# The second expert mixture of a small vision tower: rows sent through DRAM by number, or moved on the chip by 0/1 matrix products

## The chip, the cores and the metric

The kernel runs on one core of a Trainium2 chip. The metric is the time of one execution on the device in microseconds (us), as a median of several runs. Matrix products run on TensorE (PE in the profile, its weight loads as PEld), the rest on VectorE (DVE), ScalarE (ACT) and GpSimd (POOL); SyncE (SP) issues DMAs only. Each engine works off its own list of instructions in order, and semaphores tie the lists together.

## The reference

32 images of 64x64 become 17 tokens of 128 numbers each, so 544 tokens (T). Two layers follow, each of attention and a mixture of experts. The change lies in the last part, the second mixture: 32 experts, the best two for each token, and at most CAP = 43 tokens for one expert (slots are given in token order).

```python
C = int(np.ceil(CAPACITY_FACTOR * BTK / N))          # 1.25 * 1088 / 32 -> 43
probs = jax.nn.softmax(x_flat @ Wg, axis=-1)
vals, idx = jax.lax.top_k(probs, K)                  # K = 2
vals = vals / jnp.clip(vals.sum(-1, keepdims=True), 1e-09)
rank = jnp.cumsum(oh, axis=0) - oh                   # place within the expert
keep = pos < C
dest = jnp.where(keep, a * C + pos, N * C)
buf = jnp.zeros((N * C, D), x.dtype).at[dest].set(x_flat[token], mode='drop')
h = jax.nn.relu(jnp.einsum('ncd,ndh->nch', buf, W1) + b1[:, None, :])
o = (jnp.einsum('nch,nhd->ncd', h, W2) + b2[:, None, :]).reshape(N * C, D)
y_flat = jax.ops.segment_sum(gathered * w[:, None], token, num_segments=BT)
y_flat = jnp.where(contrib[:, None] <= 1e-12, x_flat, y_flat)
```

The layer's output is the residual `h` plus `y_flat`.

## The kernel before

All tokens lie on the chip in G = 5 groups g of 119 (the last of 68), tokens on the partitions: `h` is the residual, `xm[:, g, 0]` the normalised rows (`xm[:, g, 1]` a copy). The order of the work is written out by hand, per engine, in `sp`, `pool`, `act`, `dve` and `pe` blocks.

**Router stage** (about 146 to 167 us of the profile). For each group PE makes the attention's output product (`project`, 16 instructions of the profile), DVE adds it to `h` and takes the statistics (`attended`, `stats`), POOL (groups 0 and 1, by a power) or ACT (groups 2 to 4, by a root) gives the inverse deviation, DVE writes `xm` (`normalised3`), PE turns it (`router_turn`), ACT copies it out, PE makes the 32 logits (`router_logits`), DVE finds the two best and marks them (`pick2`, `mark2`), PE counts ranks (`slot_ranks`) and DVE reads the slot number off (`place2`). Between these PE runs products of a constant tile, `fill(...)`, that compute nothing that is used.

**Way out.** `scatter2` on POOL (L587) sends each row of `xm` twice, by an indirect DMA, to the DRAM buffer `rooms2` at its slot; a row carries its pair's number with it. SP waits for all ten scatters and reads `rooms2` back into `xb2` in three pieces (L480). While these are under way PE runs 32 fillers.

**Pair stage** (175 to 202 us). PAIRS = 16 pairs of experts; for each pair j PE turns the slots (`pair_turned`, L1788), DVE copies (`slots_in`, L1296), PE multiplies by the two first matrices (`pair_up`), ACT adds the bias and takes the positive part in two instructions (`rectified`, L824), PE multiplies by the two second matrices (`pair_down`), DVE adds the bias (`pair_biased`, L1301) and POOL scatters the 112 result rows to `o_rows` in DRAM (`spread_rows2`, L595).

**Way back** (203 to 214 us). SP and ACT read `o_rows` in token order (L380 to L387), DVE weights and adds the two rows of a token (L1314, L1323), five stores leave from SP and ACT (L489, L835 and others).

Every product in float32 shows as two MATMUL instructions in the trace, so a `pair_up` or `pair_down`, which is two products, shows as x4. All products made with the helper `mm` have line L1330.

## Time and profile before

| | |
|---|---|
| time, median of 3 runs | 210.02 us (209.72 to 211.75) |
| span of the profiled execution | 214.1 us, 3836 instructions |
| busy | PE 84%, PEld 63%, DVE 47%, POOL 37%, ACT 34% |
| from the first router pick to the first `pair_up` | 150.80 to 175.35 us |
| pair stage, first `pair_up` to last bias | 175.35 to 201.99 us |
| way back and stores | 202 to 214.1 us |

A time of its own is not given for the profiled execution beside its span; the span is the time from its first to its last instruction and is 4.1 us above the median of the runs. A sum of changes is therefore made on the span and then taken off or added to the median. Rows of the trace name line, engine, operation, tiles, shapes and count; the first two numbers are start and duration in us, and square brackets hold the idle time ahead on that engine and what ended it.

### The profile page before, as it was taken

The page shows a single profiled execution, that of the slowest core. Times are in us where ns is not written, and L with a number is a line of the kernel's source. Part 1 is how long each engine was busy: PE and PEld are TensorE (multiplying, and loading weights), DVE is VectorE, ACT ScalarE, POOL GpSimd, SP SyncE. Part 2 cuts the span into 40 slices and gives each one's busy share as a digit, 9 for nine tenths or more (in the row PEclk, how much of TensorE's full clock was granted, in tenths as well). Part 3 has the DMA queues.
Part 4 walks back from the last instruction along what each step waited for, and adds up shares of the span by engine and source line. Part 5 has one row for each costly group of instructions (what it writes and reads, how often), then busy time and mean ns, then how long its engine had stood idle before and what let it go on. Part 6 is the DMA issues. An engine that isn't in the chain of part 4 may idle for free.

```text
span 214.1 us, 3836 instructions
## 1 busy us (share of the span) xinstructions
PE 179.6 (84%) x1347; PEld 135.6 (63%) x1351; DVE 101.6 (47%) x373; ACT 73.2 (34%) x219; POOL 79.4 (37%) x104
## 2 busy tenths in 40 slices
PE   6979799989899899999999889968787969986400
PEld 2946467777687699999687565457664436655200
DVE  0037676978453127882217618363446713333104
ACT  2002253543425445665510554083214002332100
POOL 8008341500875037886502300001156602565510
PEclk9995999996558999999999999979999985998855
DMA  6959999980121429981140179940011153111142
GB/s 183 291 156 307 367 294 346 368 350 5 36 52 26 101 57 318 301 327 40 37 119 4 48 225 428 318 112 0 3 33 37 38 118 48 42 34 35 32 124 53
DMA packets 18956, 31.12 MB, mean 145 GB/s; under 512 B 4838, under 2 KB 12517, under 8 KB 18554
## 3 DMA queue, kind: packets, MB, share of 16 engines
q1 hardware_dynamic: 15552, 27.15, 39.5%
q0 software_dynamic: 2784, 3.31, 6.0%
q10 hardware_dynamic: 602, 0.42, 0.7%
q8 instruction: 11, 0.18, 0.3%
q14 instruction: 7, 0.06, 0.1%
HBM read 23.52 MB, written 7.40 MB: 144 GB/s over the span
## 4 chain that ended last, share of the span: by engine, by line
PE 53%; POOL 12%; DMA 12%; issue 11%; DVE 5%; ACT 2%; SPq 2%; POOLq 1%; ACTq 0%; DVEq 0%
PE ps L1330 50%; POOL rooms L587 5%; DMA patchesT<-in_patchesT 4%; POOL rooms L549 4%; DMA xb<-rooms 2%; POOL o_rows L595 2%; DVE xn L866 2%; POOL ln_rstd L525 2%; PE ps L1788 1%; DMA o_tok<-o_rows 1%; DMA rooms<-xm,slot 1%; DMA rooms<-xm,room 1%; DMA o_rows<-o_sb,result_row 1%; SPq L411 1%; PE ps L1575 1%
## 5 line engine op out<-in xcount | busy, mean ns | idle before, releaser
L556 POOL DMA_INDIRECT o_rows<-o_sb,result_row x16 | 21.0, 1312 | 18.1 <-DVE o_sb L1073 15.7
L525 POOL TENSOR_TENSOR ln_rstd<-ln_var,minus_half 119x1 f32<-119x1 f32 x12 | 6.7, 566 | 51.3 <-DVE ln_var L860 51.3
L728 ACT ACTIVATE hid_b<-ps,w_ring 128x128 f32<-128x128 f32 x64 | 18.3, 369 | 14.2 <-PE ps L1330 13.4
L595 POOL DMA_INDIRECT o_rows<-o_sb,result_row x16 | 15.1, 943 | 18.7 <-DVE o_sb L1301 15.6
L549 POOL DMA_INDIRECT rooms<-xm,room x10 | 11.4, 1144 | 15.8 <-issue 15.8
L1330 PE MATMUL ps<-w_ring,hid_b 128*128 128x128 f32 x128 | 17.0, 276 | 0.3 <-ACT hid_b L728 0.3
L1330 PE MATMUL ps<-xbT,w_ring 128*128 128x128 f32 x128 | 17.0, 275 | 0.0
L1330 PE MATMUL ps<-filler 128*128 128x512 bf16 x51 | 15.4, 433 | 1.7 <-DVE filler L878 1.5
L824 ACT ACTIVATE hid<-ps,moe_b 128x64 f32<-128x64 f32 x32 | 8.3, 311 | 24.0 <-PE ps L1330 18.6
L1330 PEld LDWEIGHTS ps<-w_ring,hid_b 128*128 128x128 f32 x128 | 15.6, 192 | 0.5 <-ACT hid_b L728 0.5
L1330 PEld LDWEIGHTS ps<-xbT,w_ring 128*128 128x128 f32 x128 | 15.6, 192 | 0.0
L1330 PE MATMUL ps<-x2T,m 128*128 128x128 f32 x64 | 12.7, 334 | 2.9 <-DVE x2T L1296 2.9
L587 POOL DMA_INDIRECT rooms<-xm,slot x10 | 11.0, 1095 | 9.5 <-DVE slot L1222 7.4
L1330 PEld LDWEIGHTS ps<-x2T,m 128*128 128x128 f32 x64 | 11.5, 251 | 3.8 <-DVE x2T L1296 3.5
L905 DVE TENSOR_TENSOR sd<-ps,decay 119x476 f32<-119x476 f32 (+1 forms) x20 | 10.8, 602 | 3.1 <-PE ps L1330 2.9
L1301 DVE TENSOR_TENSOR o_sb<-ps,moe_b 128x128 f32<-128x128 f32 x16 | 4.5, 290 | 16.3 <-PE ps L1330 14.4
L1073 DVE TENSOR_TENSOR o_sb<-ps,b_all 128x128 f32<-128x128 f32 x16 | 4.7, 291 | 15.1 <-PE ps L1330 12.4
L1330 PE MATMUL ps<-xT,w_s 128*128 128x272 f32 x32 | 11.8, 538 | 0.0
L1330 PE MATMUL ps<-w_f,heldT 128*119 128x128 f32 (+1 forms) x80 | 11.1, 297 | 0.0
L1330 PEld LDWEIGHTS ps<-filler 128*128 128x128 bf16 x55 | 6.1, 116 | 6.9 <-issue 1.7
L1330 PEld LDWEIGHTS ps<-w_f,heldT 128*119 128x119 f32 (+1 forms) x80 | 10.1, 194 | 0.4 <-issue 0.3
L613 ACT COPY xT<-ps 128x119 f32<-128x119 f32 (+1 forms) x15 | 3.6, 253 | 19.7 <-PE ps L1340 13.3
(209 smaller groups left out, 361.8 us busy)
## 6 DMA issues: line engine op xcount, KB each, us to landing
w_ring<-in_w_routed SPq DMA_DIRECT2D x16, 514.0 KB
m<-in_m SPq DMA_DIRECT2D x2, 2048.0 KB, 13.0
rooms<-zeros SPq DMA_DIRECT2D x8, 330.0 KB, 5.4
patchesT<-in_patchesT SPq DMA_DIRECT2D x6, 272.0 KB, 5.3
xb<-rooms SPq DMA_DIRECT2D x16, 66.0 KB
w_s<-in_w_s SPq DMA_DIRECT2D x2, 512.0 KB, 5.9
moe_b<-in_moe_b SPq DMA_DIRECT2D x2, 512.0 KB, 16.9
rooms<-zeros SPq DMA_DIRECT2D x1, 792.0 KB, 6.7
```

Of the source, the lines that this page charges most:

```text
L525: nc.gpsimd.tensor_tensor(ln_rstd[:, g:g + 1], ln_var[:, g:g + 1], minus_half[:], ALU.pow).then_inc(rstd_ready, 1)
L549: nc.gpsimd.indirect_dma_start(rooms[:], bass.IndirectOffsetOnAxis(ap=room[0:n, g, k:k + 1], axis=0), xm[0:n, g, k, :], None).then_inc(sca ...
L556: nc.gpsimd.indirect_dma_start(o_rows[:], bass.IndirectOffsetOnAxis(ap=result_row[:, b:b + 1], axis=0), o_sb[:, b, :], None).then_inc(o_sc ...
L587: nc.gpsimd.indirect_dma_start(rooms2[:], bass.IndirectOffsetOnAxis(ap=slot[0:n, g, k:k + 1], axis=0), xm[0:n, g, k, :], None).then_inc(sc ...
L595: nc.gpsimd.indirect_dma_start(o_rows[:], bass.IndirectOffsetOnAxis(ap=result_row2[0:past_, j:j + 1], axis=0), o2_sb[0:past_, j, :], None) ...
L728: nc.scalar.activation(hid_b[:, b % RING, c, :], ps[:, b % 2, c * BS:(c + 1) * BS], ACT.Gelu, bias=w_ring[:, b % WRING, FF + c:FF + c + 1] ...
L824: nc.scalar.activation(hid2[:, e, :], ps[:, 2 + j % 2, at:at + ROOM], ACT.Relu, bias=moe_b1[:, e:e + 1]).then_inc(hid2_ready, 1)
L866: nc.vector.tensor_scalar(xn[:, g, 0:width], h[:, g, 0:width], mv[:, g, 0:1], ln_rstd[:, g:g + 1], ALU.subtract, ALU.mult).then_inc(xn_rea ...
L905: nc.vector.tensor_tensor(sd[0:n, g % 2, r, :, :, 0:n], src, decay[0:n, r, :, 0:n].unsqueeze(2).to_broadcast([n, 2, 2, n]), ALU.mult).then ...
L1073: nc.vector.tensor_tensor(o_sb[:, b, :], ps[:, 4 + b % 2, 0:D], bias, ALU.add).then_inc(block_out, 1)
L1301: nc.vector.tensor_tensor(o2_sb[:, j, :], ps[:, 4 + j % 2, 0:D], moe_b2[:, j, :], ALU.add).then_inc(o2_ready, 1)
L1330: return nc.tensor.matmul(out_, lhsT, rhs, start=first, stop=last)
```

## The change

Rows of tokens no longer go through DRAM. What changes, part by part:

- **Slots by product.** `slots_marked` (DVE) compares, for each group, a table of slot numbers (32 experts x RS = 44 places) with each token's slot: one 119x1408 array of 0 and 1 (`in_slot`). `gather` (PE) multiplies the tokens with it, into three PSUM banks (484, 484 and 440 columns) over all groups. So that a product with 0/1 is exact, the tokens are split in two parts of type float32r, `x_hi` (ACT) and `x_lo` (POOL): 6 products a group. DVE and ACT copy the three banks to `x2T`.
- **Weights early.** The weights of a token's two experts are made group by group (`top_gap`, `gap_exponent`, `top_weights`), and `scatter2` now sends a record of 16 numbers (token number and weight) instead of a row; two loads bring the records back as `rec_in`, a row for each slot.
- **Back by product.** For pair j, ACT scales the result and rounds it (`result_high`), DVE makes the rest (`result_low`) and a 128x544 array of 0/1 from the token numbers (`tokens_marked`); PE adds both parts times that array (`pair_summed`: 238, 238, 306, 306 columns) into two PSUM banks, over all pairs, and the residual too (`residual`). One copy on DVE and one on ACT, one store each. The output is now laid out as 128x544.
- **Order of the pair stage.** Six `pair_up` and four `pair_down` come ahead; then for each j: `pair_down(j + 4)`, `pair_up(j + 6)`, `pair_summed(j)`. On ACT: `rectified(j + 6)`, `result_high(j)`. On DVE: `pair_biased(j + 4)`, `tokens_marked(j)`, `result_low(j)`.
- **Gone:** `rooms2` and its zeroing, the reload `xb2`, all turns of pairs, the 16 scatters to `o_rows` and the read back, all fillers of the stage, ACT's roots (POOL makes all five powers). **Moved or new elsewhere:** one more load on POOL's queue (`slot_base`, 4th of a row of loads near 20 us), two zeroings, two small and two broadcast loads on SP, two PSUM banks for `project`.

```diff
 (pool)
             load("room_base", room_base[:], dram["room_base"])
+            load("slot_base", slot_base[:], dram["slot_base"])
...
-            nc.gpsimd.memset(xb2[:], 0.0).then_inc(xb2_zero, 1)
+            nc.gpsimd.tensor_scalar(before16[:], before[:], 16.0, None, ALU.mult).then_inc(pool_set, 1)
+            nc.gpsimd.tensor_scalar(ones16[:], ones[:], 16.0, None, ALU.mult).then_inc(pool_set, 1)
...
+            rstd(3, (0, 1))
+            low_part(0)
+            rstd(3, (2,))
+            scatter2(0)
...
+            scatter2(3)
+            scatter2(4)
-            for j in range(PAIRS):
-                spread_rows2(j)
 (act)
-            for j in range(PAIRS):
-                rectified(j)
+            def result_high(j):
+                act.wait_ge(o2_ready, j + 1)
+                act.wait_ge(slot_w_ready, 1)
+                nc.scalar.activation(o2_hi[:, j, :], o2_sb[:, j, :], ACT.Copy,
+                                     scale=slot_w[:, j:j + 1]).then_inc(o2_hi_ready, 1)
+            for j in range(AHEAD):
+                rectified(j)
+            for j in range(PAIRS):
+                if j + AHEAD < PAIRS:
+                    rectified(j + AHEAD)
+                result_high(j)
 (dve)
+            def slots_marked(g):
+                if g >= 2:
+                    dve.wait_ge(gathered, g - 1)
+                dve.wait_ge(at_ready, g + 1)
+                nc.vector.tensor_tensor(in_slot[0:n, g % 2], slot_pos[0:n],
+                                        picked_at[0:n, g, :].unsqueeze(2).to_broadcast([n, EM, RS]),
+                                        ALU.is_equal).then_inc(in_slot_ready, 1)
+            def result_low(j):
+                dve.wait_ge(o2_hi_ready, j + 1)
+                nc.vector.scalar_tensor_tensor(o2_lo[:, j, :], o2_sb[:, j, :], slot_w[:, j:j + 1],
+                                               o2_hi[:, j, :].bitcast(F32), ALU.mult, ALU.subtract).then_inc(o2_lo_ready, 1)
+            for j in range(LATE):
+                pair_biased(j)
+            dve.wait_ge(rec_loaded, 32)
+            nc.vector.tensor_scalar(slot_w[:], rec_in[:, :, 1], row_kept[:, 0:1], None, ALU.mult).then_inc(slot_w_ready, 1)
+            for j in range(PAIRS):
+                if j + LATE < PAIRS:
+                    pair_biased(j + LATE)
+                tokens_marked(j)
+                result_low(j)
 (pe)
-            fill(FILLS, 6)
+            def pair_summed(j):
+                pe.wait_ge(of_token_ready, j + 1)
+                pe.wait_ge(o2_hi_ready, j + 1)
+                for i, own in enumerate((slice(0, SPLIT), slice(SPLIT, T))):
+                    for part in (o2_hi, o2_lo):
+                        if part is o2_lo and i == 0:
+                            pe.wait_ge(o2_lo_ready, j + 1)
+                        last = nc.tensor.matmul(ps[:, SUM_BANK[i], 0:own.stop - own.start], part[:, j, :],
+                                                of_token[:, j % CRING, own], start=j == 0 and part is o2_hi,
+                                                stop=j == PAIRS - 1 and part is o2_lo)
+            for j in range(PAIRS):
+                if j + AHEAD - 2 < PAIRS:
+                    pair_down(j + AHEAD - 2)
+                if j + AHEAD < PAIRS:
+                    pair_up(j + AHEAD)
+                pair_summed(j)
+                if 1 <= j <= G:
+                    residual(j - 1)
```

Three places of the order, as the built programs have it. First PE's pair stage. Before, pairs 3 and 4; `ps<-ident,xb` is a turn, `ps<-x2T,m` an up, `ps<-m,hid` a down, and the words in brackets are the semaphores waited for (`hid2_ready` from ACT, `x2T_ready` and `o2_ready` from DVE):

```order
L1788 MATMUL ps<-ident,xb 128x128 [waits x2T_ready]
L1330 MATMUL ps<-x2T,m 128x128 [waits hid2_ready,x2T_ready]
L1330 MATMUL ps<-x2T,m 128x128
L1330 MATMUL ps<-m,hid 64x128 [waits o2_ready,hid2_ready]
L1330 MATMUL ps<-m,hid 64x128
```

Now, the down of pair 4, the up of pair 6, the sum of pair 0, and the down of pair 5 behind it:

```order
L1412 MATMUL ps<-m,hid 64x128 [waits o2_ready,hid2_ready]
L1412 MATMUL ps<-m,hid 64x128
L1412 MATMUL ps<-x2T,m 128x44 [waits hid2_ready]
L1412 MATMUL ps<-x2T,m 128x44
L1914 MATMUL ps<-of_token,o_hi 128x238 [waits o2_hi_ready,of_token_ready]
L1914 MATMUL ps<-of_token,o_lo 128x238 [waits o2_lo_ready]
L1914 MATMUL ps<-of_token,o_hi 128x306
L1914 MATMUL ps<-of_token,o_lo 128x306
L1412 MATMUL ps<-m,hid 64x128 [waits o2_ready,hid2_ready]
```

The turns are gone, and between two ups there now stand products that wait for ACT and DVE; a product of the sum is one instruction here, not two.

Second, ACT in the same stage. Before, all 32 halves of `rectified` in a row:

```order
L824 ACTIVATE hid<-ps,moe_b 128x64 [waits up2_done]
L824 ACTIVATE hid<-ps,moe_b 128x64
L824 ACTIVATE hid<-ps,moe_b 128x64 [waits up2_done]
L824 ACTIVATE hid<-ps,moe_b 128x64
L824 ACTIVATE hid<-ps,moe_b 128x64 [waits up2_done]
```

Now, pairs 6 and 7 with the high parts of pairs 0 and 1:

```order
L866 ACTIVATE hid<-ps,moe_b 128x44 [waits up2_done]
L866 ACTIVATE hid<-ps,moe_b 128x44
L873 ACTIVATE o_hi<-o_sb,slot_w 128x128 [waits slot_w_ready,o2_ready]
L866 ACTIVATE hid<-ps,moe_b 128x44 [waits up2_done]
L866 ACTIVATE hid<-ps,moe_b 128x44
L873 ACTIVATE o_hi<-o_sb,slot_w 128x128 [waits slot_w_ready,o2_ready]
```

Behind each pair's two halves now stands the high part of the pair six places back.

Third, DVE in the router stage, from the ranks of group 1 to the pick of group 2. Now:

```order
L1262 TENSOR_TENSOR place_of<-marks,ps 119x64 [waits rank2_done]
L1265 TENSOR_TENSOR picked_at<-place_of 119x32 [waits dve_step]
L1268 TENSOR_REDUCE slot<-place_of 119x2
L1292 TENSOR_SCALAR gap_sum<-gap 119x1 [waits gap_exp]
L1293 RECIPROCAL rec<-gap_sum 119x1 [waits dve_step]
L1294 TENSOR_TENSOR rec<-gap,rec 119x1 [waits dve_step]
L1278 TENSOR_TENSOR in_slot<-slot_pos,picked_at 119x1408 [waits at_ready]
L1246 MAX top<-ps 119x8 [waits logits_done]
```

Before, `place_of`, `slot` and the next pick stood there; the rows L1265, L1292 to L1294 and L1278 are new between them.

## Rows read from the trace of the kernel before

**Rows 1.** The page: span, and TensorE's granted clock in 40 slices.

```profile
span 214.1 us, 3836 instructions
PEclk9995999996558999999999999979999985998855
```

**Rows 2.** Timeline, 19 to 24 us: DVE beside POOL's loads.

```profile
19.84 3.43 DVE L866 TENSOR_SCALAR xn<-h,mv,ln_rstd 119x128 f32<-119x128 f32 x1 [0.17 <-POOL ln_rstd L525]
20.34 0.53 POOL L498 DMA_DIRECT2D ones<-in_ones  x1
21.36 1.82 POOL L560 MEMSET probs<- 128x2048 f32 x1
```

**Rows 3.** Timeline of the router stage.

```profile
150.80 0.20 DVE L1202 MAX8 top<-ps 119x8 f32<-119x32 f32 x1 [1.42 <-PE ps L1330]
153.56 0.19 DVE L1218 TENSOR_TENSOR place_of<-marks,ps 119x64 f32<-119x64 bf16 x1
162.24 0.30 ACT L668 COPY xm<-xm 119x128 f32<-119x128 f32 x1
```

**Rows 4.** Groups by form, DVE: busy us, mean ns.

```profile
L1091 DVE TENSOR_TENSOR q_mixed<-w_t,th_q 128x1024 f32<-128x1024 f32 x4 | 4.9, 1218 | 0.0
L1076 DVE TENSOR_TENSOR w_t<-w_t 128x1524 f32<-128x1524 f32 x1 | 1.7, 1728 | 0.0
L893 DVE TENSOR_SCALAR kT<-xT,parity 128x544 f32<-128x544 f32 x2 | 0.9, 500 | 0.7 <-ACT xT L613 0.7
L895 DVE COPY qT<-ps 128x544 f32<-128x544 f32 x1 | 0.7, 724 | 1.1 <-PE ps L1330 1.1
L1323 DVE SCALAR_TENSOR_TENSOR ymoe<-o_tok,pair_w,h 119x128 f32<-119x128 f32 x4 | 1.4, 345 | 0.0
```

**Rows 5.** Timeline: 512 columns in bf16 (29 in a row) and in float32.

```profile
166.05 5.96 PEld L1330 LDWEIGHTS ps<-filler 128*128 128x128 bf16 x29
104.83 3.60 PE L1330 MATMUL ps<-q_mixed,w_t 128*128 128x512 f32 x8
```

**Rows 6.** Timeline of the records' model: last scatter, reload, first turn.

```profile
169.39 1.11 POOL L587 DMA_INDIRECT rooms<-xm,slot  x1 [0.30 <-issue]
172.30 2.79 SPq L480 DMA_DIRECT2D xb<-rooms  x6
174.63 0.20 PEld L1788 LDWEIGHTS ps<-ident,xb 128*128 128x128 f32 x2 [1.98 <-DMA xb<-rooms]
```

**Rows 7.** Timeline of the pair stage at half clock.

```profile
180.10 0.70 PE L1330 MATMUL ps<-m,hid 128*64 128x128 f32 x4
180.73 0.48 PE L1788 MATMUL ps<-ident,xb 128*128 128x128 f32 x1
181.00 1.06 PE L1330 MATMUL ps<-x2T,m 128*128 128x128 f32 x4
182.10 0.52 ACT L824 ACTIVATE hid<-ps,moe_b 128x64 f32<-128x64 f32 x2 [1.37 <-PE ps L1330]
```

**Rows 8.** The same at full clock.

```profile
184.31 0.44 PE L1330 MATMUL ps<-m,hid 128*64 128x128 f32 x4
184.68 0.33 PE L1788 MATMUL ps<-ident,xb 128*128 128x128 f32 x1
184.85 0.61 PE L1330 MATMUL ps<-x2T,m 128*128 128x128 f32 x4
185.50 0.52 ACT L824 ACTIVATE hid<-ps,moe_b 128x64 f32<-128x64 f32 x2 [0.56 <-issue]
187.49 0.29 DVE L1301 TENSOR_TENSOR o_sb<-ps,moe_b 128x128 f32<-128x128 f32 x1 [2.15 <-PE ps L1330]
```

**Rows 9.** Engines by stretch: us, PE busy (count), granted clock, DMA share, GB/s.

```profile
190.00:194.00 4.00, 2.67 (x23) 1.00 0.15 43
194.00:198.00 4.00, 3.66 (x24) 0.75 0.12 33
```

**Rows 10.** Timeline: the last store.

```profile
211.83 0.36 ACTq L837 DMA_DIRECT2D out_h<-ymoe  x1
```

More of the change, by code:

```diff
@@ L55 @@
 ROOM = 64
+RS = 44
 TAKEN = 48
@@ L427, in _ @@
                              zeros[:, 0:n * RW]).then_inc(rooms_zero, 16)
+            for half in range(2):
+                at = (1 + half) * HALF_STEP
+                sp.dma_start(rec_rows[at:at + TAKEN * REC, :].rearrange("(p r) c -> p (r c)", p=128),
+                             zeros[:, 0:TAKEN * REC * REC // 128]).then_inc(rooms_zero, 16)
             sp.dma_start(w2_s[:], dram["w2_s"]).then_inc(shared_loaded, 16)
@@ L785, in _, with high_part @@
             folded_out(1)
-            nc.scalar.activation(warm[:], eps_col[0:1, 0:1], ACT.Sqrt)
             for grp in range(2, GRPS):
                 held_to(grp)
-            def deviation3(g):
-                act.wait_ge(aggr_ready, 3 * G + g + 1)
-                nc.scalar.activation(ln_std[:, g:g + 1], mv[:, g, 1:2], ACT.Sqrt, bias=eps_col[:, 0:1]).then_inc(std_ready, 1)
+            def high_part(g):
+                n = rows(g)
+                act.wait_ge(xn_ready, 3 * G + g + 1)
+                nc.scalar.copy(x_hi[0:n, g, :], xm[0:n, g, 0, 0:D]).then_inc(hi_ready, 1)
             def router_out(g):
@@ L1231, in _ @@
             softmaxed(3)
+            here(dve, "row_kept", "rec")
             attended(0)
@@ L1317, in _ @@
[L1317 to L1324 removed]
+                nc.vector.tensor_tensor(o2_sb[:, j, :], ps[:, DOWN_BANK[j % 2], 0:D], moe_b2[:, j, :],
+                                        ALU.add).then_inc(o2_ready, 1)
@@ L1706, in slot_ranks, with gather @@
                 pe.wait_ge(picks_ready, G + g + 1)
-                mm(dst, ones[0:1, 0:n], room_base[:, ER:], True, False)
+                mm(dst, ones[0:2, 0:n], slot_base[:], True, False)
                 for f in range(g):
                     for k in range(2):
-                        mm(dst, ones[:, 0:n], marks2[:, f, k, :], False, False)
+                        mm(dst, ones16[:, 0:n], marks2[:, f, k, :], False, False)
                 pe.wait_ge(pick_marked, G + g + 1)
                 for k in range(2):
-                    last = mm(dst, before[0:n, 0:n], marks2[0:n, g, k, :], False, k == 1)
+                    last = mm(dst, before16[0:n, 0:n], marks2[0:n, g, k, :], False, k == 1)
                 last.then_inc(rank2_done, 1)
+            def gather(g):
+                n = rows(g)
+                pe.wait_ge(hi_ready, g + 1)
+                pe.wait_ge(lo_ready, g + 1)
+                if g == 0:
+                    pe.wait_ge(held_out, GRPS)
+                pe.wait_ge(in_slot_ready, g + 1)
+                for i, bank in enumerate(GATHER_BANKS):
+                    own = slice(i * BANK_OF_EXPERTS, min((i + 1) * BANK_OF_EXPERTS, EM))
+                    width = (own.stop - own.start) * RS
+                    for part in (x_hi, x_lo):
+                        last = mm(ps[:, bank, 0:width], part[0:n, g, :],
+                                  in_slot[0:n, g % 2, own, :].rearrange("p e r -> p (e r)"),
+                                  g == 0 and part is x_hi, g == G - 1 and part is x_lo)
+                    if g == G - 1:
+                        last.then_inc(gathered, 1)
+                if g < G - 1:
+                    last.then_inc(gathered, 1)
             mixed(0)
```

399 lines of the change are left out of this document (222 added, 177 removed).

## The prediction, made before the changed kernel was timed

> **What bounds the kernel now.** I read the table of stages first, then the page's span and clock, then the timeline from 145 us on, and the groups by form for prices. Only the last 70 us and one place near 20 us are touched. The span is 214.1 us [rows 1]. The stage's first router pick stands at 150.80 [rows 3], the last scatter of a row at 169.39, and the first turn can only run at 174.63, because the rows go out to DRAM and back [rows 6]. Then 16 pairs run to 202 us. Read off the starts in [rows 8], a pair takes 0.37 us for the down (184.31 to 184.68), then turn and up, 1.07 us in all at full clock. Part of the stage runs at half clock (about 1.88 us a pair, [rows 7]), and there are waits like the 2.15 us in [rows 8], in which DVE stands although PE's product is over. The last 12 us are scatter, read back, ten additions and stores, with PE idle. The change takes aim at both DRAM trips; the question is what the on-chip way costs in order.
>
> **1. The start: +0.5 us.** POOL's loads near 20 us and its memset behind them stand in the way of DVE's last normalisation: it starts at 19.84, beside the first load, and takes 3.43 us where the usual is a third of a microsecond, until the memset is over (21.36 + 1.82) [rows 2]. One more load in that row costs its 0.53 us [rows 2], and PE waits for the normalisation. The zeroings and small loads on SP lie far ahead of their use; the two broadcasts come behind the last weights, 10 us or so before the first compare. I cost these at nothing.
>
> **2. Router stage: about 0.5 us shorter.** Group 0 reaches its slot at 153.56 as before [rows 3]; with the two new small operations and the three of the weights the first compare starts at 154.2. DVE now carries a period: compare, 1408 elements at the rate of 1024 in 1.218 and 1524 in 1.728 us [rows 4], so 1.61; pick, marks and gap about 0.9; normalise, add, statistics, variance 1.1; place, slot and weights about 1.0. Operations that don't wait for each other overlap by some 0.1 us, so 4.5 us for groups 0 to 2, and 3.9 where no attention product is left. Compares start at 154.2, 158.7, 163.2, 167.1 and 170.9, and the last ends at 172.5. PE's share of a period (project 1.9, gather, turn, logits, ranks) fits in it if the gather is short.
>
> **The price of a float32r product** stands in no row. A float32 instruction moves 512 columns in 0.43 us (8 in 3.60 with one end of 0.6), a bf16 one in 0.21 (29 in 5.96) [rows 5]: 0.84 and 0.41 ns a column. The two ends are these, or even 1.7 ns, both instructions of a float32 product. I take 0.41: the program issues one instruction where float32 has two, and it splits every number in two parts, which would be pointless if the product kept all bits. The Trainium skill (FP8 and Floating Point Precision, TensorE Precision Notes) says that true float32 is four passes and that a reduced form reads 4 bytes and truncates; one pass of four would be the same 0.41, so the sum by it is the sum here, where the nearest row alone would give 0.84 and the second rival's time. No run here has shown it yet.
>
> With 0.41, a gather is 2816 columns, 1.2 us. The last ends near 174.1, the copies of 484 columns take 0.64 (724 ns for 544, [rows 4]), and the first up starts at 174.9, where it was 175.35.
>
> **3. Waiting for the records: first sum at 181.8.** The last weights are ready at 173.0, two scatters start 1.4 us apart (173.2, 174.6), and from the last scatter's start to the reload is 2.91 us, from there to use 2.33 [rows 6]: 179.8, and the weights of the slots at 180.0. PE meanwhile runs 7 ups and 5 downs, each down waiting for ACT: about 0.8 us a pair, up(6) at 180.0. Then comes ACT's pair 6, the high part of pair 0, the low part, the sum: 181.8. So the shorter first trip is mostly used up again: the wait for a landed row is replaced by a wait for a landed record.
>
> **4. The pair loop: the main term.** The order rows ahead show a ring. sum(j) on PE waits for the low part (DVE), which waits for the high part (ACT), which stands behind both halves of rectified(j + 6), which waits for up(j + 6), which stands on PE behind down(j + 4) and behind sum(j - 1). So each of these runs after the other, once a pair, while there are ups left. Full clock, step by step:
> - down: 0.37 (184.31 to 184.68) [rows 8];
> - up until ACT starts: 0.65 (184.85 to 185.50) [rows 8], less 84 columns at 0.84 ns in its last instruction, 0.58;
> - two halves on ACT: 0.52 [rows 8];
> - high part: 0.30, as a copy of 128 from SBUF [rows 3];
> - low part: 0.35 (345 ns for this form) [rows 4];
> - the other three products, 238 + 306 + 306 columns at 0.41 ns: 0.35;
> - two hops between engines: 0.1.
>
> That is 2.57 us; PE's own work in it is only about 1.3, DVE's 1.0 (0.29 bias, 0.50 for a 544 compare [rows 4], 0.35), both beside the ring. Nine periods from sum(0) to sum(9), 23.1, and five residuals of 0.22, 1.1: 206.0. Two periods without an up (down, bias, compare, low part) of 2.1: 210.2. Four more at DVE's 0.7: 213.0. Last sum, copy, store: 0.4 + 0.2 + 0.45 + 0.1, and 2.3 from issue to the end (211.83 to 214.1) [rows 10, 1]: 216.4. With the start's 0.5: **216.9, or +2.8 us, at full clock throughout.**
>
> **5. The clock.** Half clock is granted in part of the stage today (4 us around 194 to 198 at 0.75) after a stretch in which PE was busy 2.67 of 4 us [rows 9]. The new ring keeps PE busy about half the time, and the fillers that held the clock are gone. At half clock a period has down 0.63 (180.10 to 180.73) and up 1.10 less 0.14 [rows 7], sum 0.70: 3.6 us instead of 2.57. Over the whole loop, with ups ahead, gathers and tail, that is about +17. I take something under a third of the stage: +5. **Span 221.8, +7.7; on the median 210.0 that is 217.7, say 217.5 us.** The span and the median differ by 4.1 us before, and I assume the same after.
>
> **Rivals.**
> - *Half clock throughout* (chance 0.12). For: a ring with gaps in every period; against: the clock held through 190 to 194 [rows 9]. 216.9 + 17 - 4.1: 230 us.
> - *float32r at the rate of a float32 instruction* (0.10). Gathers of 2.4 us on PE's path make the first up 3.5 us later, and each of 11 periods gains 0.36, with the last four and sum(0) near 9 us in all: 221.5 us. At 1.7 ns it would be above 240.
> - *Full clock throughout* (0.17): 212.8 us.
> - *The ring's hops overlap* (0.21), the one on the other side. Place: the pair loop. My steps are durations laid end to end; if ACT and DVE start before the record in front of them ends, or the shorter ups return sooner, a period comes to 2.0 us. Then 11 periods save 6.3: span 210.6, 206.5 us. It decides from a period of 2.3 down, since 2.8 / 11 is 0.25. For: waits like DVE's 2.15 us in [rows 8], in which nothing had to be waited for, are in the old sum and not in the new one. Against: up to relu, 0.65, is read as it stands.
> - The forecast, ring at about 3.0 us a period, has the rest, 0.40.
>
> That the change leaves a DRAM trip in place is in the sum: records and stores.
>
> **Range and chances.** The forecast's own range is 213.5 to 222. To leave out 2 in 10 I go down to 206, which takes in most of the fast case, and up to 229. About 1% of the time is what a measurement of this kernel can tell: faster than 207.9 has 0.20 (nearly all of the overlap case), within 207.9 to 212.1 has 0.14 (its rest and the low half of the full-clock case), slower has 0.66.
>
> **What would show it.** First up near 175 and first sum near 182; the sum's starts 2.6 to 3.6 us apart for pairs 0 to 9, then closer; ACT and DVE idle more than half of each period, PE waiting for `o_lo`; the granted clock below 1 somewhere after 182; a 484-column product in 0.2 us; DVE's normalisation near 20 us at 3.9. I am wrong if the sums come every 1.4 us (PE's work alone), if the first up is later than 178, or if the records land after 183.

## The result: 236.9 us where 217.5 was forecast

The changed kernel takes 236.86 us (median of 4 runs, 233.43 to 239.60), the kernel before 210.17 (4 runs, 209.72 to 211.75). Where the executions of a kernel fall into groups by time, here and below, a ratio is that of the faster ones; here it is 1.114, 95% interval 1.104 to 1.125. The direction was forecast, the size was not: the time lies 8 us above the range's end, 229. The profile is of the longest of the four executions, with a span of 237.8 us.

```profile
span 237.8 us, 3985 instructions
PEclk9988999955599999999999979589555555555557
```

These two lines of the page answer to [rows 1]. A digit stands for 5.9 us. From the 29th digit on, which begins at 166.5 us, all but the last read 5: half clock until the last few us. The last ten digits of the kernel before are 9985998855.

The rest is read from the timeline of the changed kernel. First the start, which answers to [rows 2]:

```profile
19.57 0.35 DVE L914 TENSOR_SCALAR xn<-h,mv,ln_rstd 119x128 f32<-119x128 f32 x1 [0.21 <-POOL ln_rstd L547]
21.08 0.52 POOL L519 DMA_DIRECT2D slot_base<-in_slot_base  x1
21.59 1.82 POOL L583 MEMSET probs<- 128x2048 f32 x1
21.73 2.43 DVE L941 TENSOR_SCALAR kT<-xT,parity 128x544 f32<-128x544 f32 x2 [1.82 <-ACT xT L646]
```

The normalisation that was held for 3.43 us takes 0.35 here; the operation behind it is held instead, and `kT` is done at 24.16, before it was at 24.92. The stage itself, which answers to [rows 3, 4]:

```profile
149.10 0.20 DVE L1246 MAX8 top<-ps 119x8 f32<-119x32 f32 x1 [1.60 <-PE ps L1412]
153.89 1.62 DVE L1278 TENSOR_TENSOR in_slot<-slot_pos,picked_at 119x1408 fp32r<-119x1408 f32 x1
163.42 2.04 POOL L547 TENSOR_TENSOR ln_rstd<-ln_var,minus_half 119x1 f32<-119x1 f32 x1
```

And two pieces of the gathers, at full and at half clock. The first number of a row is its start, and what one product costs is the distance of two starts:

```profile
157.57 0.38 PE L1412 MATMUL ps<-in_slot,x_lo 119*128 119x484 f32 x1
157.79 0.38 PE L1412 MATMUL ps<-in_slot,x_hi 119*128 119x484 f32 x1
...
171.48 0.61 PE L1412 MATMUL ps<-in_slot,x_hi 119*128 119x484 f32 x1
171.88 0.61 PE L1412 MATMUL ps<-in_slot,x_lo 119*128 119x484 f32 x1
```

A float32r product of 484 columns costs 0.22 us at full clock (0.45 ns a column) and 0.40 at half (0.83). Then the records, answering to [rows 6], and the first sum:

```profile
175.52 0.70 PE L1412 MATMUL ps<-x2T,m 128*128 128x44 f32 x3
175.65 1.11 POOL L617 DMA_INDIRECT rec_rows<-rec,slot  x1 [0.31 <-issue]
177.99 0.80 SPq L509 DMA_DIRECT2D rec_in<-rec_rows  x2
183.09 0.23 DVE L1399 TENSOR_SCALAR slot_w<-rec_in,row_kept 128x16 f32<-128x16 f32 x1
186.44 0.54 PE L1914 MATMUL ps<-of_token,o_hi 128*128 128x238 f32 x1 [0.95 <-ACT o_hi L873]
```

One period of the pair loop, to be held against [rows 7]:

```profile
187.76 0.70 PE L1412 MATMUL ps<-m,hid 128*64 128x128 f32 x4
188.39 0.93 PEld L1412 LDWEIGHTS ps<-x2T,m 128*128 128x128 f32 x4 [0.33 <-issue]
188.39 1.08 PE L1412 MATMUL ps<-x2T,m 128*128 128x44 f32 x4
189.51 0.49 ACT L866 ACTIVATE hid<-ps,moe_b 128x44 f32<-128x44 f32 x2 [3.21 <-PE ps L1412]
189.89 0.40 ACT L873 ACTIVATE o_hi<-o_sb,slot_w 128x128 fp32r<-128x128 f32 x1
190.32 0.35 DVE L1386 SCALAR_TENSOR_TENSOR o_lo<-o_sb,slot_w,o_hi 128x128 fp32r<-128x128 f32 x1 [1.11 <-ACT o_hi L873]
190.43 0.54 PE L1914 MATMUL ps<-of_token,o_hi 128*128 128x238 f32 x1 [0.96 <-ACT o_hi L873]
192.16 0.70 PE L1412 MATMUL ps<-m,hid 128*64 128x128 f32 x4
```

The order is the forecast ring: down, up, two rectifyings, high part, sum (the next down at 192.16 stands behind a residual of 0.41). As long as there are ups, the first product of a sum waits for ACT's high part. Sums are 3.99 us apart without a residual and 4.40 with one. The last stretch, answering to [rows 9, 10]:

```profile
186.00:220.00 34.00, 26.23 (x106) 20.38 (x106) 8.44 (x24) 6.32 (x26) 0.00 (x0) 0.50 0.00 0
220.00:238.00 18.00, 12.14 (x48) 9.53 (x48) 6.53 (x19) 3.33 (x11) 0.00 (x0) 0.58 0.05 15
...
235.50 0.40 ACTq L885 DMA_DIRECT2D out_h<-yT  x1
```

PE is busy 26.2 of 34 us, all at half clock, and POOL has nothing to do.

The 16.0 us between the forecast span, 221.8, and the measured one, 237.8, stand as follows. The first pick is 2.2 early (149.1, with the start's 0.5 expected at 151.3). From it to the first up are 26.4 us where 24.1 were forecast. From there to the first sum 10.9, forecast 6.9. From the first sum to the end 51.4, forecast 34.6 at full clock plus 5 for the clock. On the median 3 us more: it is only 0.9 below the span here, where 4.1 was assumed.

That assumption mixed two things. One execution takes 1.8 us more than its span here (239.6 and 237.8), and about 2.2 more in the kernel before (211.32 and 209.2, timed beside fill_router). The 4.1 the other way came of the execution that was profiled: with a span of 214.1 and a mean granted clock of 0.886 it was longer than every execution of the kernel before that is listed with its span (205.8 to 213.2). So [rows 1] show less clock than that kernel mostly has.

### The profile page after: what moved, and what is told of

The parts are those of the page before. It is cut to its first block, busy times and chain, and to the rows that moved or that the text cites. A ratio compares the mean times of both kernels' runs of the same rounds, so it can differ in the third digit from the quotient of the medians.

```text
span 237.8 us, 3985 instructions
## 1 busy us (share of the span) xinstructions
PE 208.2 (88%) x1398; PEld 164.6 (69%) x1398; DVE 116.1 (49%) x402; ACT 75.9 (32%) x235; POOL 73.2 (31%) x100
## 4 chain that ended last, share of the span: by engine, by line
PE 80%; ACT 6%; DVE 5%; DMA 4%; issue 3%; SPq 1%; DVEq 0%; ACTq 0%
PE ps L1412 70%; PE ps L1914 9%; DMA patchesT<-in_patchesT 4%; ACT o_hi L873 1%; ACT hid L866 1%; DVE kT L941 1%; ACT heldT L794 1%; SPq L437 1%; PE ps L1657 1%; DVE in_slot L1278 1%; ACT hid_b L761 0%; PE ps L1422 0%; ACT xT L831 0%; DVE of_token L1393 0%; ACT xT L646 0%
## 5 line engine op out<-in xcount | busy, mean ns | idle before, releaser
L579 POOL DMA_INDIRECT o_rows<-o_sb,result_row x16 | 20.9, 1304 | 18.3 <-DVE o_sb L1121 15.8
L1914 PE MATMUL ps<-of_token,o_hi 128*128 128x238 f32 (+1 forms) x32 | 15.7, 490 | 11.2 <-ACT o_hi L873 9.6
L547 POOL TENSOR_TENSOR ln_rstd<-ln_var,minus_half 119x1 f32<-119x1 f32 x15 | 10.0, 668 | 39.5 <-DVE ln_var L908 39.3
L866 ACT ACTIVATE hid<-ps,moe_b 128x44 f32<-128x44 f32 x32 | 7.8, 294 | 37.9 <-PE ps L1412 37.9
L1914 PEld LDWEIGHTS ps<-of_token,o_hi 128*128 128x128 f32 x32 | 10.1, 316 | 13.2 <-issue 10.8
L1412 PEld LDWEIGHTS ps<-x2T,m 128*128 128x128 f32 x64 | 15.0, 325 | 4.7 <-issue 3.3
L1412 PE MATMUL ps<-x2T,m 128*128 128x44 f32 x64 | 17.0, 423 | 0.0
L1914 PE MATMUL ps<-of_token,o_lo 128*128 128x238 f32 (+1 forms) x32 | 15.2, 477 | 0.0
L617 POOL DMA_INDIRECT rec_rows<-rec,slot x10 | 12.1, 1214 | 6.1 <-DVE rec L1294 4.1
L1412 PE MATMUL ps<-w_f,heldT 128*119 128x128 f32 (+1 forms) x80 | 13.5, 338 | 0.0
L1412 PE MATMUL ps<-m,hid 128*64 128x128 f32 x64 | 11.1, 449 | 0.0
```

The costliest lines, as they stand in the source:

```text
L547: nc.gpsimd.tensor_tensor(ln_rstd[:, g:g + 1], ln_var[:, g:g + 1], minus_half[:], ALU.pow).then_inc(rstd_ready, 1)
L579: nc.gpsimd.indirect_dma_start(o_rows[:], bass.IndirectOffsetOnAxis(ap=result_row[:, b:b + 1], axis=0), o_sb[:, b, :], None).then_inc(o_sc ...
L617: nc.gpsimd.indirect_dma_start(rec_rows[:], bass.IndirectOffsetOnAxis(ap=slot[0:n, g, k:k + 1], axis=0), rec[0:n, g, k, :], None).then_inc ...
L866: nc.scalar.activation(hid2[:, e, 0:RS], ps[:, UP_BANK[j % 2], ROOM * half:ROOM * half + RS], ACT.Relu, bias=moe_b1[:, e:e + 1]).then_inc( ...
L1412: return nc.tensor.matmul(out_, lhsT, rhs, start=first, stop=last)
L1914: last = nc.tensor.matmul(ps[:, SUM_BANK[i], 0:own.stop - own.start], part[:, j, :], of_token[:, j % CRING, own], start=j == 0 and part is ...
```

## The experiments

Each was timed beside the kernel before on the same chip; ratios are against it, with 95% intervals. Two chips were in use: fill_router, fill_all, ring_open, ring_open_fill and the last three experiments ran on one, all other experiments on another. In the table a span is cut at the first router pick, at the first up and at the first sum, because what lies ahead of the pick is the same program in all variants of the change and yet ended anywhere from 145.2 to 150.7 us.

| kernel | pick to up | up to sum | sum to end | a period |
|---|---|---|---|---|
| forecast, full clock | 24.1 | 6.9 | 34.6 | 2.57 |
| changed kernel | 26.4 | 10.9 | 51.4 | 3.99 |
| fill_router | 23.5 | 9.5 | 50.9 | 3.98 |
| fill_all | 24.2 | 13.7 | 41.0 | 2.87 |
| ring_open | 25.2 | 9.8 | 36.7 | 2.71 |
| ring_open_fill | 23.6 | 13.2 | 24.4 | 1.52 |
| ahead7_one (fallen) | 25.4 | 13.5 | 34.7 | 2.71 |
| ahead7 | 23.7 | 8.9 | 22.8 | 1.52 |
| hold_fill | 23.9 | 8.9 | 22.8 | 1.51 |

A period is read without a residual. The theory: two causes, the half clock (A) and the ring's order. The rivals: one of them alone.

### The clock

**fill_router.** Filler products in the router stage only, into the bank of the attention product that is free at that time:

```diff
             router_turn(0)
+            pe.wait_ge(h_joined, 3 * G + 1)
+            fill(3, OUT_BANK[0])
             router_logits(0)
...
             router_logits(3)
+            fill(4, OUT_BANK[1])
             slot_ranks(3)
```

> The changed kernel with filler products (512 columns, bf16) put back into the router stage only: 3 after the first turn, 1 after each later one, 4 and 2 ahead of the last two ranks; the pair stage is as it was. Theory A (the clock: nearly all of the +26.7 us is the half clock from 166.7 us on, and it fell because PE stood idle near 148 to 150 and 164 to 166): the granted clock stays 1.00 from 150 to 175, the router stage ends 2 to 3 us earlier (first up near 173), but nothing holds the clock in the pair stage, so a first up at 173 and still half clock behind it: 232 to 235 us. If instead one fall is all that matters and the clock stays up by itself once it is up, the pair stage runs at full clock and the ring gives 2.57 us a period: near 218 us. Rival B (the clock is not the cause, the order of the ring is): 236 to 238 us, no change.

233.87 us, ratio 1.105 (1.098 to 1.112). The stage to the first up is 2.9 us shorter and its clock is 1.00, but the clock falls behind it and the loop keeps its 3.98 us a period: half clock from 175 to 230 us. The stage's own loss is small; nothing held the clock where the time is.

**fill_all.** Fillers in the waits of the pair stage as well:

```diff
                 pair_up(j + 2)
+                fill(1, 3)
...
+                fill(6 if j == 0 else 3, 3 if j == 0 else 6)
                 pair_summed(j)
...
+                            fill(1, 6)
                             pe.wait_ge(o2_lo_ready, j + 1)
```

> As fill_router, and fillers in the pair stage as well: one behind each of the first four ups, six while PE waits for the records, then in each pair three ahead of the sum and one between its high and its low product, all where PE waits anyway. The ring of waits is untouched. Theory A: granted clock 1.00 from 150 us to the end, the sums 2.57 us apart (2.5 to 3.0) in place of 3.99, first up near 173, first sum near 182, and 215 to 219 us. Rival B (the ring costs what it costs whatever the clock, or fillers stand in its way): sums 3.5 to 4 us apart and 232 us or more. If the clock stays low in spite of the fillers, they cost 0.43 us each in part of the waits: 240 us.

227.33 us, ratio 1.074 (1.066 to 1.083): 9.5 us less than the changed kernel, 8 to 12 short of what theory A said. The clock still fell between 168 and 185; from 186 on it is 1.00, and the ring can be read at full clock:

```profile
205.55 0.35 PE L1927 MATMUL ps<-of_token,o_hi 128*128 128x238 f32 x1 [0.31 <-ACT o_hi L873]
206.45 0.44 PE L1412 MATMUL ps<-m,hid 128*64 128x128 f32 x4
206.82 0.64 PE L1412 MATMUL ps<-x2T,m 128*128 128x44 f32 x4
207.50 0.48 ACT L866 ACTIVATE hid<-ps,moe_b 128x44 f32<-128x44 f32 x2 [2.09 <-PE ps L1412]
207.87 0.40 ACT L873 ACTIVATE o_hi<-o_sb,slot_w 128x128 fp32r<-128x128 f32 x1
208.42 0.35 PE L1927 MATMUL ps<-of_token,o_hi 128*128 128x238 f32 x1 [0.31 <-ACT o_hi L873]
```

The sums are 2.87 us apart, of which 0.2 is the filler between high and low product: 2.67 against the forecast 2.57. So the clock alone is not the cause: at full clock a period of the ring is still 2.67 us, where the open ring below needs 1.52. In the last sums, where nothing has to be waited for, the fillers cost (1.40 a sum, 0.68 without them).

**before_no_fill.** The kernel before without its fillers.

```diff
             router_turn(0)
-            fill(1, 3)
             router_logits(0)
...
-            fill(FILLS, 6)
```

> The kernel before with its 10 small fillers of the router stage and the 32 ahead of the first turn left out, nothing else. If the clock of its last 60 us hangs on them (theory A: what the change lost is largely what the fillers held), the granted clock falls near 150 and stays low through the router stage and the pairs: the router stage's PE work of about 20 us at half clock in part hidden, 16 pairs at about 1.9 us in place of 1.1 to 1.9: 214 to 222 us. If its turns and ups hold the clock by themselves, 209 to 212 us.

212.16 us, ratio 1.016 (1.000 to 1.032). The clock did fall, and it hardly mattered: behind 165.95 PE only waits for rows, and then the pairs came back to full clock near 182.

```profile
174.15 0.66 PE L1780 MATMUL ps<-ident,xb 128*128 128x128 f32 x2 [8.20 <-DMA xb<-rooms]
```

The fillers were worth about 1.6% to the kernel before, between nothing and 3.2%.

**before_more_fill.** Ten fillers more ahead of its first turn.

```diff
-FILLS = 32
+FILLS = 42
```

> The kernel before with 42 fillers ahead of its first turn in place of 32, so that they end at about 174.6, when the rows are in, and not at 172.5; nothing else. If the idle 2 us ahead of the first turn bring the half clock of 176 to 182, it stays at full clock there and the pairs end 3 to 4 us earlier: 206.5 to 208 us. If the fall comes of the pairs' own gaps, no change within 1 us. It says how much of a faster version's lead over the kernel before is the clock alone.

209.16 us, ratio 0.998 (0.992 to 1.004), no change, where 206.5 to 208 was expected if the fillers held the clock. Its profile does show full clock in every stretch of the pairs. But there was less to gain than [rows 1] suggest: its four executions had a mean clock of 0.913 to 0.930, the seven of the kernel before beside it 0.885 to 0.929, with 0.917 in the middle. What sets their pace then is POOL; its scatters to DRAM, from the timeline:

```profile
185.48 0.94 POOL L595 DMA_INDIRECT o_rows<-o_sb,result_row  x1 [0.30 <-issue]
186.73 0.94 POOL L595 DMA_INDIRECT o_rows<-o_sb,result_row  x1 [0.30 <-issue]
187.98 0.94 POOL L595 DMA_INDIRECT o_rows<-o_sb,result_row  x1 [0.30 <-issue]
```

One each 1.25 us, without a gap, while PE was through before 192 and the last scatter began at 195.46. In the kernel before a part of PE's loss at half clock was hidden by that queue. The change took the queue away and put PE on the path.

### The ring

**ring_open.** No fillers; ACT and DVE do what belongs to the sum first:

```diff
 (act)
+                result_high(j)
                 if j + AHEAD < PAIRS:
                     rectified(j + AHEAD)
-                result_high(j)
 (dve)
+                tokens_marked(j)
+                result_low(j)
                 if j + LATE < PAIRS:
                     pair_biased(j + LATE)
-                tokens_marked(j)
-                result_low(j)
```

> The changed kernel without any filler, but the ring cut: ScalarE makes the high part of pair j before it rectifies pair j + 6, and VectorE does the compare and the low part of pair j before the bias of pair j + 4. The sum of pair j then waits for nothing that the same period has begun. Theory A with the clock at half: PE bounds the loop, down 0.63, up about 0.7 and four sums of about 1.2, 2.5 us a pair where 3.99 were: 10 periods save about 15 us, 222 us; and if the fuller PE brings the clock back, 1.3 to 1.6 us a pair and 208 to 213 us. Rival (the products themselves or the hops are the cost, and the order is not): 233 us or more.

219.88 us, ratio 1.032 (1.023 to 1.042): 17.0 us for two exchanges of lines. The stretch 186 to 200:

```profile
186.00:200.00 14.00, 14.00 (x64) 11.86 (x64) 4.60 (x14) 3.86 (x15) 0.00 (x0) 0.50 0.00 0
```

PE is busy all of it, and bounds, at 2.71 us a pair. The clock had fallen at 164 and stayed at half all the same, without a ring, until only sums were left near 215.

**ring_open_fill.** The same with the router stage's fillers, one behind each of the first four ups and six ahead of the first sum.

> The cut ring of ring_open with the fillers of the router stage, one behind each of the first four ups and six ahead of the first sum; none in the loop. Both causes taken away: clock 1.00 from 150 us to the loop, first up near 173, first sum 181, and then PE bounds at 1.3 to 1.6 us a pair: the loop ends near 205, the kernel at 204 to 209 us, at or below the kernel before. If the clock falls in the loop in spite of a full PE: 2.5 us a pair and near 218 us. If filling alone does it and the order adds nothing, it equals fill_all.

210.53 us, ratio 0.989 (0.981 to 0.997), less than 2% below the kernel before and 1.5 us over the expected 204 to 209. The clock was at half from 173 to 186.6, and 1.00 behind it; periods of 1.52. The four kernels make a square, though not with the same fillers in both rows (fill_all has four in every period, this one none): opening the ring takes 17.0 us without fillers and 16.8 with them, the fillers 9.5 with the ring closed and 9.4 with it open. Both causes are real, and here they add. The changed kernel was timed in a session of its own, in which the kernel before was 1.1 us faster, so the agreement of the differences is good to about 1 us only.

**act_order_only.** ring_open_fill with DVE's order as in the changed kernel (bias first).

> ring_open_fill with ScalarE's order changed alone: the high part of pair j ahead of the rectifying of pair j + 6, VectorE's order as in the changed kernel (bias of pair j + 4, compare, low part). What is left of the ring: sum(j - 1), down(j + 4) 0.37, bias 0.29, compare 0.49, low part 0.35, the low products 0.3 and a hop: 1.8 to 1.9 us a pair where ring_open_fill had 1.52 (1.73 with a residual) and fill_all 2.87 (3.09 with one). Over ten periods that is 1 to 3 us more than ring_open_fill: 211.5 to 213.5 us. If the link through ScalarE's rectifying was the whole ring, it equals ring_open_fill, 210.5.

221.79 us, ratio 1.054 (1.044 to 1.064): 8 us above the expected range. The link through ACT was not the whole ring. Through DVE it is 2.3 us with a residual at full clock, where ring_open_fill has 1.73; and the clock fell in the loop at 199 and a period became 2.78. The two causes may be tied: this ring makes gaps again (PE is busy 11.61 of the 13 us from 186 to 199), and the gaps would cost the clock too. That is argued, not shown: in fill_all PE is busy 17.15 of the 19 us from 186 to 205, the same share, and the clock stays 1.00.

### The record trip, and how far ahead

**no_record_wait.** ring_open_fill with the records loaded early from zeros, so without the second mixture in the result:

```diff
-            sp.wait_ge(scattered2, 16 * 2 * G)
...
-                             rec_rows[at:at + TAKEN * REC, :].rearrange("(r j) c -> r (j c)", j=PAIRS)).then_inc(rec_loaded, 16)
+                             zeros[0:TAKEN, 0:PAIRS * REC]).then_inc(rec_loaded, 16)
```

> ring_open_fill with the records loaded ahead of the router stage from a zeroed tile, so that slot weights and token numbers are there at once (the result is then without the second mixture; every instruction stays). It prices the trip that the change left in DRAM. In ring_open_fill slot_w was written at 180.50 and the first sum stood at 185.32, behind pairs ahead and six fillers at half clock. If the record trip bounds: first sum 4 us or more earlier and 206 us. If PE's work ahead of the first sum at half clock bounds (the in-order place of the sum behind six ups, four downs and ten fillers): first sum still within 1 us of 185, and the time within 1 us of 210.5.

210.19 us over ten runs, ratio 1.000 (0.993 to 1.006) against 0.989 of ring_open_fill; the first sum still 13.7 us behind the first up. The trip bounds nothing here: PE's own work ahead of the sum does. In ahead7 and hold_fill below, where the first sum stands 4 us nearer to the first up, the trip was not tested again.

**ahead9, ahead11, ahead7, ahead7_one.** ring_open_fill with three fillers ahead of the first up, n ups ahead of the loop (one more comes in it ahead of the first sum), two fillers behind each from the third on (one in ahead7_one), none just ahead of the sum. The cut is that of ahead7:

```diff
-AHEAD = 6
-LATE = 4
+AHEAD = 7
+LATE = 5
...
+            fill(3, 3)
             pair_up(0)
...
                 pair_up(j + 2)
+                fill(2, 3)
```

> As ring_open_fill, but nine pairs of ups and seven of downs (6 and 4 before) ahead of the first sum, three fillers ahead of the first up, two behind each up ahead of the sums (one before), and none of the six ahead of the first sum. In ring_open_fill the first up started at 172.08, the clock fell at about 173.5 to half and came back near 186.5, and the first sum stood at 185.32. If the clock can be held there, a pair ahead takes 1.1 to 1.3 us, seven more are done by 182, the first sum comes at 182 and the 16 sums, 7 ups and 9 downs behind it at PE's rate take about 18 us: 204 to 206 us. If the clock falls all the same, a pair ahead takes 2.3 us or more and the first sum comes near 188 with less left behind it: 208 to 211 us, the same as ring_open_fill.

> As ahead9 with eleven ups and nine downs ahead. The records can be had at about 180; pairs ahead of that time are free, later ones only move work from behind the first sum to ahead of it. Theory: the same as ahead9 within 1 us at full clock. If VectorE's backlog (compares 0.49, low parts 0.35) bounds the end when more of PE's work is ahead, the end stays at 16 x 0.85 to 1.0 us behind the first sum: at most 1 us faster than ahead9, and 1 to 3 us slower where the clock is at half ahead of the sums.

> ahead9 with seven ups and five downs ahead of the first sum, two fillers behind each up there as before. In ahead9 the records are read from 173.25 on, so can be had near 176.4, the first sum stood at about 181, and each pair ahead of it takes 1.37 us with 0.43 us of fillers in it. With seven the sums start near 178; two pairs with four fillers less: 0.9 us faster than ahead9 if the clock holds, 203 to 205 us as the median; where it falls, 208 to 212 us.

> ahead7 with one filler behind each up ahead of the sums in place of two. ring_open_fill had one and fell to half clock near 173.5, but without the three ahead of its first up. If the fall came from the wait ahead of the first up, this holds and is 0 to 1 us faster than ahead7. If it comes from the gaps between ups, downs and ScalarE, the clock falls at about 173 again and it takes 208 to 211 us.

| kernel | single times, us | ratio of the faster group |
|---|---|---|
| ahead9 | 203.45, 204.81, 209.08, 229.02 | none given |
| ahead11 | 204.28, 204.84, 205.74, 226.40 | 0.978 (0.961 to 0.995) |
| ahead7 | 202.82, 203.14, 225.34, 225.65 | 0.969 (0.961 to 0.977) |
| ahead7_one | 204.79, 206.01, 220.64, 226.17 | 0.980 (0.972 to 0.989) |

How many pairs are ahead matters little. What matters is that the same program now runs at 203 or at 225. A fallen execution was expected at 208 to 212 us and takes 220 to 229: none of these kernels has the six fillers in a row behind which the clock of ring_open_fill came back. Both groups have a profile, ahead7 at 202.82 and ahead7_one at 226.17. The first pick stands 5.05 us later in the second, so the same work lies in the stretches 160.95 to 166.95 and 166.95 to 172.95 of ahead7:

```profile
160.95:166.95 6.00, 4.54 (x33) 3.15 (x32) 5.68 (x17) 0.82 (x4) 5.43 (x5) 1.00 0.03 3
166.95:172.95 6.00, 5.38 (x35) 3.87 (x37) 4.26 (x17) 1.92 (x8) 4.58 (x4) 1.00 0.06 6
```

and 166 to 172 and 172 to 178 of ahead7_one:

```profile
166.00:172.00 6.00, 4.54 (x32) 3.14 (x32) 5.68 (x17) 0.82 (x4) 5.44 (x5) 1.00 0.03 3
172.00:178.00 6.00, 5.65 (x19) 4.27 (x21) 3.76 (x15) 1.11 (x4) 4.54 (x4) 0.50 0.06 6
```

Up to the fall the two are the same: PE idle 1.5 of 6 us, at full clock. Behind it the clock is at half in one, and stays there until 220 us, and at 1.00 in the other. So this much idleness does not settle which way an execution goes.

### A version that keeps the clock

**hold_fill.** ahead7 with PE's last idle places of the router stage filled:

```diff
             gather(3)
+            fill(3, 3)
             gather(4)
...
-            fill(3, 3)
+            fill(4, 3)
             pair_up(0)
```

> ahead7 with three fillers more ahead of the last gather, where TensorE waits for VectorE's compare (0.82 us of idle in ring_open_fill's row), and four ahead of the first up (three before). In ahead7_one's profile TensorE was busy 4.54 of the 6 us from 166 to 172 and the clock fell to half behind that, to the end. If those idle stretches bring the fall, every execution now holds the clock: 203 to 205 us, none near 225. If the fall has another source, some executions still take 220 us or more.

205.78 us (204.47 to 208.17, six runs), ratio 0.977 (0.969 to 0.985), 2.3% below the kernel before. The interval leaves out no change at all, but not a gain just under 2%. No execution was near 225, where the four kernels without these fillers had 6 of 16 at 220 or more; at that rate, six good ones in a row would come by luck 6 times in 100.

```profile
166.00:175.00 9.00, 7.68 (x50) 5.06 (x48) 8.58 (x28) 1.54 (x6) 7.87 (x7) 1.00 0.05 6
175.00:186.00 11.00, 11.00 (x85) 7.21 (x85) 4.78 (x17) 4.58 (x19) 1.39 (x2) 1.00 0.05 11
186.00:196.00 10.00, 10.00 (x82) 8.20 (x82) 6.08 (x19) 4.65 (x18) 0.00 (x0) 1.00 0.01 2
```

**burst_fill.** hold_fill with 12 fillers ahead of the first up, in place of 4.

> As hold_fill with 12 fillers ahead of the first up in place of 4. A burst is what stood ahead of each return of the clock to full (in ring_open_fill at about 186.5, behind six fillers in a row; in ring_open, without one, only at about 214). At full clock the eight more cost 8 x 0.21 = 1.7 us, less what was waiting: 204 to 206.5 us. Where the clock had fallen in the router stage it comes back behind the burst, at 176 or so, and such an execution takes 208 us and not 225. If executions near 225 are seen all the same, a burst does not bring the clock back.

**loop_fill.** hold_fill with one filler ahead of each sum.

> As hold_fill with one filler ahead of every sum in the loop (16 in all). TensorE bounds the loop, so they cost 0.21 us each at full clock: 16 x 0.21 = 3.4 us, 206.5 to 208.5 us where hold_fill has 203 to 205. If the clock falls in spite of the fillers ahead, they bring it back within the loop: no execution over 218 us. If they neither cost nor hold anything, it equals hold_fill.

burst_fill 207.35 us (205.37 to 210.24), ratio 0.983 (0.975 to 0.991); loop_fill 207.37 (205.42 to 208.64), ratio 0.983 (0.975 to 0.991). burst_fill is 0.85 us over its expected range; its eight fillers cost the 1.7 us they add (25.6 us from pick to up in the profile, 23.9 in hold_fill). loop_fill is where it was expected partly by luck: hold_fill was slower than thought and the 16 fillers cost 1.6 us and not 3.4; a period grew by 0.15 (1.66 against 1.51). None of their executions was near 225 either, which makes 18 of 18 with the fillers of hold_fill.

A rival is left: all three kernels ran on one chip, and all four that had fallen executions on the other. Neither group was run on both, so it is not shown that the fillers, and not the chip or the session, kept the clock. Since none of their executions fell, the last two don't tell either whether a burst would have brought the clock back. The profiles that show a return behind six fillers in a row are ring_open_fill, fill_all, act_order_only and no_record_wait, between 184.7 and 186.9 us.

## Why the prediction failed, step by step

- **The clock (step 5): this is the step that failed.** It took "something under a third of the stage" at half clock, +5 us, and the loop's whole length ran at half: the three stretches behind the first pick were 23.1 us longer than forecast at full clock (2.3, 4.0 and 16.8). It was judged from [rows 9], where PE, busy 2.67 of 4 us, kept 1.00, and the case of half clock throughout got a chance of 0.12. But in [rows 1] the slice from 176.6 to 182.0 already reads 5, with fillers ahead of it, the change took all fillers out, and the forecast ring was to leave PE idle half the time. Each of these spoke for the rival. Neither ring nor missing fillers are the whole of it. Without fillers the old order was back at 1.00 near 182 (before_no_fill). Without fillers the new one stayed at half even with the ring open (ring_open, 164 to 215). With fillers up to the first up and the ring closed it fell at 175 and stayed there (fill_router). It came back early only where the pair stage had fillers too.
- **The price of half clock** was low too: the rival said 230. It had +17 us for the 23.1 above. A period was put at 3.6 us and measured 3.99. Up to ACT's start takes 1.12 us and not 0.96: with 44 columns in place of 128 an `up` is no shorter (1.08 us against 1.06 in [rows 7], and 0.64 against 0.61 in [rows 8]); its four weight loads, the PEld row above, take 0.93 of it. Sum and low part took 1.32 us and not 1.05. A residual costs 0.41 at this clock, and 0.22 as forecast only at full.
- **The ring (step 4)** was right in its order and its size: 2.67 us measured at full clock in fill_all, 2.57 forecast. The single steps were less right: 0.68 to ACT's start (forecast 0.58), rectifying 0.37 (0.52, since the high part starts before the record ahead of it ends), high part to product 0.55 (0.40 with a hop). Too much and too little cancelled, which is luck. PE waited for `o_hi` and not, as named, for `o_lo`, whose product starts 0.33 us later. The rival of overlapping hops, 0.21, was wrong in its result: ACT does start before the record ahead of it ends, and the longer up and the later first product take it back.
- **float32r (step 2)** at one pass: 0.45 ns a column measured, 0.41 taken. The second rival falls.
- **The router stage:** compares at 153.9, 159.0, 163.4, 167.3 and 171.3, forecast 154.2 to 170.9. That agreement is luck, since the first pick was early: counted from it they start 4.8 to 22.2 us on, where 3.4 to 20.1 was forecast and fill_router has 3.7 to 19.8. 24.1 us from pick to up was forecast for full clock, and 23.5 to 23.9 were measured where the clock held that far (25.6 in burst_fill, with its twelve fillers). fill_router, with the clock at 1.00, is 2.9 us shorter than the changed kernel here, so the 2.3 us over the forecast are the half clock again.
- **The records (step 3):** last scatter to reload 2.34 us, forecast 2.91. They were not what the first sum waited for: `slot_w`, on DVE behind the bias of pair 3, was written at 183.09, and no_record_wait gains nothing. The first sum at 186.4 and not 181.8 is PE at half clock ahead of it, 1.64 us a pair where 0.8 was put down. I had named the wrong bound: with seven ups and five downs in front of the sum, the trip is covered at this clock.
- **The span and the median:** 4.1 us apart was taken over from one profile and was 0.9 here, as the section on the result says; 3.2 us of the miss are this term.
- **The start (step 1)** can't be told: the pick stands between 145.2 and 150.7 us in profiles of the same code ahead of it, more than the 0.5 at stake. What was to be held was not: `xn` took 0.35 us in the changed kernel.

What stays open is what makes the clock fall near the last gather in one execution and not in the next. With the idle places filled none of 18 executions fell, which agrees with idleness as the cause, but on another chip than those that fell; and the profiles of ahead7 and ahead7_one show the same idleness ahead of a clock that stays and one that falls.

## What to carry to other kernels

Before a change takes fillers or a DMA queue out of a stage, ask which engine paces it afterwards. If that is TensorE, the clock enters the sum in full, and a forecast should price both levels to the end of the kernel; here the low one had a chance of 0.12 and every execution of the changed kernel ran at a mean clock of 0.79 to 0.83. A span from one profile should be set beside the spans of other executions before a difference to the median is carried over. And when a result takes part in a loop on three engines, write down for each engine what the sum of pair j stands behind: here two exchanges of lines were worth 17 us, more than the largest gain seen over the kernel before, about 7 us in the faster executions of ahead7.

## What the runs showed of the hardware

- **A busy TensorE can stay at half clock.** In ring_open it is busy 14.00 of 14 us, with products of 44 and 128 columns, weight loads and four products of the sum a pair, and the granted clock stays 0.50. Nearly the same work at full clock keeps it there (hold_fill, 10.00 of 10 at 1.00). The Trainium skill (TensorE: Matmul & The Clock Gate, What's actually happening) says that the gate follows how busy the array has been; the share that the profile calls busy was not enough to see it by, as it was 1.00 in both. Returns were seen behind six fillers of 512 columns (four profiles), in ring_open when only sums of 238 and 306 columns were left, and, in the kernel before, between [rows 7] and [rows 8] with no filler at all, where turn and up are 128 columns wide and not 44.
- **Which level a run gets can be chance:** ahead7 took 202.8, 203.1, 225.3 and 225.7 us. Four runs of one kernel may miss the other level.
- **float32r** costs 0.45 ns a column at 484 columns (0.22 us) and 0.49 at 306 (0.15 us between starts).
- **POOL beside a DVE comparison with two inputs from SBUF:** the power of 119 values, 0.55 to 0.59 us elsewhere in the stage, took 2.04 us when it started beside the compare of 1408 elements at 163.42, longer than the compare itself (1.61). fill_router, ahead7 and hold_fill each show it once too, 2.05 us.
